# First attention layer: one step more between scores and transposes, and the query and key split one step earlier

## The reference

```python
Q = (x @ Wq.T).reshape(b, n, H, R)        # x layer-normed, H = 8 heads, R = 64
K = (x @ Wk.T).reshape(b, n, H, R)
V = (x @ Wv.T).reshape(b, n, H, d)        # d = 128
attn = softmax(einsum('bnhr,bmhr->bhnm', Q, K), axis=-1)      # no scale
out = einsum('bhnm,bmhd->bnd', attn, V)                       # summed over heads
x = x + out + experts_of_layer_0(xn)
```

## Time and profile before

| | us |
|---|---|
| median of 3 runs | 1496.58 (1493.58 to 1497.97) |
| profiled execution, its own time | 1496.05 |
| its span | 1494.3 |
| first layer (about) | 36 to 420 in the span |
| second layer | 455 to the end |

### The profile page before, as it was taken

How to read it: one execution, slowest core, us unless ns; L and a number is a source line. 1 busy time by engine, 2 the same in 40 slices (tenths; PEclk the granted TensorE clock), 3 DMA queues, 4 the chain that set the end, 5 groups by cost and what they waited for, 6 DMA issues and landing times.

```text
span 1494.3 us, 25209 instructions
## 1 busy us (share of the span) xinstructions
PE 1229.9 (82%) x6185; PEld 575.0 (38%) x6185; DVE 1280.2 (86%) x3505; ACT 1158.9 (78%) x1324; POOL 789.9 (53%) x1166
## 2 busy tenths in 40 slices
PE   2798687878864788899888988899888998899887
PEld 1476455555541233333333333333333333333333
DVE  5686687878866689999999999999999999999997
ACT  1566576767725689998899899998899998998960
POOL 2702100000000278878788777888788877887730
PEclk7899899999977799999999999999999999999998
DMA  5002200000000000000000000000000000000001
GB/s 183 13 1 34 16 1 0 0 0 0 0 1 18 7 19 26 19 18 21 26 23 18 18 28 25 18 18 18 28 25 18 18 28 25 18 18 18 28 25 32
DMA packets 38780, 31.58 MB, mean 21 GB/s; under 512 B 6150, under 2 KB 35609, under 8 KB 38738
## 3 DMA queue, kind: packets, MB, share of 16 engines
q1 hardware_dynamic: 37714, 29.76, 6.7%
q0 software_dynamic: 1024, 1.35, 1.0%
HBM read 29.10 MB, written 2.75 MB: 21 GB/s over the span
## 4 chain that ended last, share of the span: by engine, by line
DVE 30%; PE 26%; issue 9%; DVEq 3%; ACT 1%; POOL 0%; ACTq 0%
DVE arena L1024 17%; PE ps L1304 9%; PE ps L1317 7%; DVE arena L1010 6%; PE ps L1361 4%; PE ps L1381 2%; PE ps L1353 2%; DVE x L1067 2%; PE ps L1335 2%; DVE z L1050 2%; DVE spread L1076 1%; DVE nmax L1016 1%; DVEq L1023 1%; DVEq L1067 1%; ACT arena L1161 1%
## 5 line engine op out<-in xcount | busy, mean ns | idle before, releaser
L1024 DVE SCALAR_TENSOR_TENSOR arena<-arena,ps 128x512 f32<-128x512 f32 x1024 | 663.1, 679 | 65.9 <-PE ps L1317 65.7
L1161 ACT ACTIVATE arena<-arena,eps 128x4096 f32<-128x4096 f32 x128 | 474.3, 3709 | 38.6 <-POOL arena L1284 38.1
L1317 PE MATMUL ps<-spread,sel 128*128 128x512 f16 x1024 | 348.5, 386 | 118.4 <-DVE arena L1024 112.1
L1278 POOL TENSOR_SCALAR arena<-kT,negq 128x512 f32<-128x512 f32 x480 | 331.6, 701 | 196.5 <-DVE arena L1024 181.3
L1284 POOL TENSOR_SCALAR arena<-arena,q 128x512 f32<-128x512 f32 x480 | 351.8, 743 | 22.4
L1304 PE MATMUL ps<-arena,phi_cols 128*32 128x512 f32 x2048 | 276.4, 614 | 20.2 <-ACT arena L1161 20.2
L1317 PEld LDWEIGHTS ps<-spread,sel 128*128 128x128 f16 x1024 | 92.1, 97 | 513.0 <-DVE arena L1024 438.4
L1149 ACT ACTIVATE arena<-kT,q 128x512 f32 (+1 forms) x330 | 217.8, 715 | 3.0
L489 ACT ACTIVATE kT<-ps,region 128x512 f32<-128x512 f32 x128 | 88.2, 689 | 101.3 <-DVE region L559 97.7
L1270 POOL TENSOR_SCALAR negq<-q 128x256 f32<-128x256 f32 x4 | 3.5, 870 | 297.6 <-POOLq L762 297.6
L1010 DVE TENSOR_SCALAR arena<-kT,q 128x512 f32 (+1 forms) x214 | 141.9, 686 | 0.3 <-PEq L762 0.3
(11 more groups left out here) (196 smaller groups left out, 1794.9 us busy)
## 6 DMA issues: line engine op xcount, KB each, us to landing
wge<-in_e_wg SPq DMA_DIRECT2D x32, 256.0 KB, 2.7
w1e<-in_e_w SPq DMA_DIRECT2D x32, 128.0 KB, 2.1
w2e<-in_e_w SPq DMA_DIRECT2D x32, 128.0 KB, 2.1
w3e<-in_e_w SPq DMA_DIRECT2D x32, 128.0 KB, 2.1
region<-in_w SPq DMA_DIRECT2D x1, 2048.0 KB
out<-x SPq DMA_DIRECT2D x4, 256.0 KB, 2.7
region<-in_wqk SPq DMA_DIRECT2D x1, 512.0 KB, 4.6
region<-in_wv SPq DMA_DIRECT2D x1, 512.0 KB, 5.3
```

Source lines behind the costliest of these rows:

```text
L1024: dve.scalar_tensor_tensor(feat[:, j, k, :], feat[:, j, k, :], 1.0, psB[:, k % BANKS, :], ALU.mult, ALU.mult, accum_out=sums[:, j, gg, c:c ...
L1161: act.activation(grp, grp, ACT.Sqrt, bias=eps[:]).then_inc(e_ready, 2)
L1278: pool.tensor_scalar(feat[:, j, QUADS * gg + c, :], kT[:, b * N:(b + 1) * N], HUGE, negq[:, b % 2, at - b * N // 2:at - b * N // 2 + 1], A ...
L1317: pe.matmul(psB[:, k % BANKS, :], sel[:, gg, c, :], spread[:, j, :], start=True, stop=True).then_inc(bc_done, 1)
```

## The change

The split of queries and keys (projection on PE, high parts on ACT, low parts on DVE) moves from steps 1, 2, 3 of a head to steps 0, 1, 2. The transposes, the low parts of the transposes and the value products follow the scores by 3, 4 and 5 steps instead of 2, 3 and 4. The output of a row is therefore copied, transposed and added one step later, and the drain has 9 steps instead of 8. No instruction is added or removed but for that empty step.

```diff
-        QK_AT, QK_HI, QK_LO = 1, 2, 3
-        LAG_T, LAG_LO, LAG_W = 2, 3, 4
+        QK_AT, QK_HI, QK_LO = 0, 1, 2
+        LAG_T, LAG_LO, LAG_W = 3, 4, 5
...
-        OUT_AT = 5
+        OUT_AT = 6
         DRAIN = OUT_AT + 3
```

## The result

| | before | after |
|---|---|---|
| median of 3 runs, us | 1496.58 | 1536.98 (1533.86 to 1541.0) |
| profiled execution, us | 1496.05 | 1541.0 |
| span, us | 1494.3 | 1538.9 |

What follows compares the result with a forecast made beforehand. Waits between PE and DVE, going in lockstep, were taken to bound the kernel. Rows 13.5, row 0 4, starts 2.7 and drain 1.2 made 21.4; with 6 for the clock, 1496.05 became 1523.5, say 1524, range 1507 to 1545.

Steps and rivals of the forecast that it cites:

- The clock's term: PE idling 2.8 us in step 2 of each head: three more clock falls of 2 us, +6, bounds 0 and 56.
- The two couplings: DVE's row maximum needs PE's scores; PE's transposes need the bank pT_lo frees; a step costs the larger engine's work.
- step 0 of a head: Heads 4 to 6: 3.19 us forecast instead of 2.5; staying near 2.5 would mean PE gets ahead of DVE.
- The rows at full clock: Each row costs +4.5 us through the misfit of steps; rows 1 to 3 together +13.5.
- DVE's long step: Step 2 of heads 4 to 6, DVE's scaling plus `keep_qk_lo`: 1.79 + 1.45 = 3.24 us, against 0.93 for PE.
- Row 0: First row, with few value products to delay in heads 0 and 1: +4 us taken, bounds 0 and 5.
- The row start: From a row's last row maximum to the next row's first: 8.4 us instead of 7.49, three starts +2.7.
- My second sign of being wrong: First layer: PEclk falling well under the 0.96 of before would show the prediction wrong.
- The reason I gave for few falls: PE's 2.8 us idle per head is shorter than the idle that led to a fall once, so three more falls.
- The rule of the Trainium skill: Matmul groups separated by short PSUM waits make the clock swing; falls in most heads, 1565 us; that rival's chance 0.12.
- 1545 by a dozen: Rival that the clock falls in most heads: 1545 us with a dozen falls, 1557 to 1574 by full count; chance 0.12.
- The rival of a faster kernel: Extra lag decouples the engines, step 3 falls from 3.76 to 2.50 in 12 heads: gain 15, 1481 us; chance 0.08.

Runs made afterwards that it cites:

- the two parts alone: Against the kernel before: only the split moved to steps 0 to 2, ratio 1.0540; only lags 3, 4, 5 and output at step 6, ratio 1.0358.
- filled gaps: Changed kernel plus three unread matmuls in step 3 of every head but head 1, and at the starts, of rows 1 to 3: 1510.06 us, ratio 1.0187.
- value products at 6: Changed kernel with value products 6 steps behind the scores instead of 5, output at step 7, fifth value projection at step 10: 1490.13 us, ratio 1.0045.
- scores first: Changed kernel with head 1 projected behind the scores at a row's first step, instead of ahead of transposes and scores: 1540.53 us, ratio 1.0316.
- the fitted one: Changed kernel, value products 6 steps behind scores, head 1 projected behind scores at row starts, later value projections in DVE's long step: 1485.74 us, ratio 0.9939.

## Why the prediction was right, and where it was off

The mechanism held and the direction with it. The clock's term was far too small, and the stall hid some 7 us of what it cost. That part is luck: without it the time would have been near 1544 (an estimate, 1537 and 7), at the edge of the range.

- **The two couplings.** PE's wait for pT_lo and DVE's for the scores set every step, and step 0 of a head did not stay near 2.5. Shown by the head at full clock (3.13, 2.30, 3.36, 1.36 against 3.19, 2.33, 3.24, 1.36), and by the two parts alone, whose steps follow the same rule where the clock is full. L660's wait for `keep_qk_lo` fell from 19.3 us in 17 places to 1.2 in one, as forecast.
- **The rows at full clock.** +4.5 a row was forecast; the changed schedule with filled gaps gives +5.1. The difference is DVE's long step, 3.36 instead of 3.24. Row 0 was +3.2, for +4, but with unequal stalls; without a stall it took 97.3 (the kernel before with extra matmuls at the start of rows 1 to 3) and 102.4 (the changed kernel with filled gaps, none of them in row 0), so +5.
- **The row start.** 8.4 forecast, 8.52 at full clock, 10.1 to 10.5 measured. Moving the projection does not help, as shown.
- **The clock: the term that was mis-sized.** "Three more falls of 2: +6". Rows 1 to 3 and their starts lost 35.7, where the full-clock schedule loses 3 x 5.1 + 3 x 1.0 = 18.4. The rest, 17, is the clock less what the larger stall of before and its one fall take off. Against the kernel with filled gaps, rows 2 and 3 lost 6.6 and 5.5 to the clock and the three starts 5.3; with 6 for row 1 (an estimate, from rows 2 and 3) that is some 23, nearly four times the forecast. My second sign of being wrong, PEclk in the layer well under 0.96, came true: it was 0.89.
- **Where the rest of the misfit lies.** The spans differ by 44.6 where 27.4 were forecast (the medians by 40). Of these 17, 11 are the clock's rest above, 2 the rows and starts at full clock, 3 what lies behind the last row maximum, and 1.7 what lies ahead of the first; row 0 takes 1 off.
- **The reason I gave for few falls** was that 2.8 of idle is shorter than the 3.09 which led to a fall only once. It did not hold: the extra matmuls remove the falls and 0.9 to 1.3% of the time. The rule of the Trainium skill that was weighed (TensorE: Matmul & The Clock Gate, A second HAM failure mode: psum-queue depth-cycling) pointed the right way, and the trace agrees in part, with the clock at 0.89 over the layer. But the clock fell in part of the heads, and it did not go with the number of short waits. In row 2 PE waited for pT_lo 10 times before, up to 1.2 us, and 16 times with the value products at 6, up to 1.6 us, both at a clock of 1.00; in the changed kernel it waited 8 times, up to 2.8 us, at 0.92.
- **A slip in the rivals.** "1545 by a dozen" falls should be 1517.5 + 12 x 2 = 1541.5; nothing else rests on it.
- **The rival of a faster kernel.** Removing the waits it counted on did happen inside the heads (L543's wait for k_hi was 14.4 us in 5 places, all but 0.3 of it at the four row starts, instead of 21.1), and bought nothing, because the step that replaced them is longer. What the lag of the transposes is worth can't be told from nothing (1.5 us).
- Not settled: why the clock fell behind one gap of 2.73 and not behind another (heads 5 of row 1 and 4 of row 2 show the same gap), what the stall is, and the 1.7 us up to the first row maximum. The projection ahead of the scores may be a part of these: on one chip the first row maximum was at 40.63 in the changed kernel and 38.64 and 38.84 in two kernels with scores first, but 41.59 in the third, and for the kernel before 38.59 and, with its extra matmuls on another chip, 42.02.

## What to carry to other kernels

Where two engines release each other once a step, as PE and DVE here, with the release at the end of one's step and ahead of the other's long work, they go in lockstep, and a schedule costs the sum over the steps of the larger of the two: put the heavy pieces of both engines in the same step, and write the sums down before moving a lag. A wait that disappears from the list of waits is no gain if the step it stood in is replaced by a longer one. And a schedule with the same work but one long gap of TensorE had a second price here, the clock at which the work behind the gap runs; a few matmuls that nobody reads, put into the gap, tell the two prices apart.

## What the runs showed of the hardware

- A gap of 2.7 to 2.8 us of PE inside a busy loop was enough for the granted clock to fall to 0.61 over the next 4 us in part of the heads. With only the lags changed it fell behind waits of 1.2 and 2.1 us close together (0.59 from 330 to 334). With waits of up to 1.6 us (value products at 6) it stayed at 1.00 over the row. It could also fall behind shorter ones: at the end of row 2 of the kernel before they were 1.16 and 0.69, with PE busy for 2.29 of 4 us, and 0.57 followed.
- Three unused float32 matmuls of 0.86 us in these gaps, all but head 1's, kept it at 1.00 over a whole row of 84 us, at 0.98 over the two others, and shortened the kernel by about 1%.
- In two comparisons DVE stood still in rows 0 and 1 for what the profile calls remote, in every kernel profiled (14.7 us in the kernel before, 12.2 in the fitted one), in two others in none; the kernel before took 1496 in the former and 1482 to 1483 in the latter.
- DVE's subtraction into partitions 64 to 127 started 0.52 us behind the scaling ahead of it (316.80 to 317.32 in the trace after), where pT_lo in the same place started 0.40 behind (162.39 to 162.79 in the trace before); why wasn't tried. It is the 0.12 by which step 2 was longer than forecast.
